# Both value-matmul groups of an attention unit placed side by side in layer 0

## Chip, cores, metric

One core of one Trainium2 chip runs the whole program. The metric is device time in microseconds (us), the median of several executions of one compiled kernel. The profile and the trace come from one execution, taken by the hardware profiler.

## What is computed

Two transformer layers with parallel branches, on x of 4 sequences x 256 tokens x 512 features, in float32:

```python
xn = layernorm(x)
x = x + attn0(xn) + ffn0(xn)      # 32 query heads, 8 key/value heads, head size 16, no mask
xn = layernorm(x)
x = x + attn1(xn) + ffn1(xn)      # same head layout, rotary positions, causal mask
```

`attn0` is softmax(q k^T / 4) v for every head, then a 512x512 output projection. The change touches only this attention.

## The kernel before

The four sequences are n = 0..3 in layer 0. The 32 heads of a sequence are cut into S = 4 slices of 8 heads, so layer 0 has 16 **units** u = 4n + s. A unit is worked in eight **slots**, i = 0..7. In slot i three things can stand on TensorE:

- `("st", u, i)`, L785: transposed scores of 128 keys against 2 heads x 256 queries, into PSUM bank `k % 3` (banks 0 to 2). ScalarE then writes exp of it to `probs[:, i]` (L953). Slots 0 to 3 hold the first 128 keys, slots 4 to 7 the second 128.
- `("m", u + 2, i)`, L752: scores of the unit two ahead, for the row maximum only. VectorE reduces them (`neg_max`, L1097). These scores go to one of the three work banks 3, 4, 5, which rotate among all short-lived products, so a matmul for a work bank waits until VectorE or ScalarE has read what stood there three products ago.
- one piece of **beside** work, from `beside_units`: projections of the next sequence (`qkv`), output projection of the previous one (`wo`), transposes of normalised input (`xn`), value transposes (`v`), and weight splits (`split`) on ScalarE and VectorE.

The **value matmuls** `("pv", u, t)`, L813, multiply `probs` by the values. Group t = 0 uses probs 0 to 3, group t = 1 uses probs 4 to 7; both accumulate in one bank, 6 or 7 by the parity of u. A group is four 128-row by 32-column matmuls on four column strips of the array, and float32 makes each two passes, so the trace counts 8. Before a group the program waits for the last exp that it reads. ScalarE's exps of unit u wait in turn for group t of unit u - 1, because they overwrite its `probs`:

```python
if u:
    act.wait_ge(pv_done, 2 * (u - 1) + t + 1)
```

Once per unit come two more small steps. `("mt", u + 1)`, L766, transposes the maxima, VectorE copies them (`max_t`, L1106), and a DMA (`mrow`, L554) puts them in a row of `big`, on which score step 0 of that unit waits. `("norm", u - 1, k)`, k = 0..3, in slots 4 to 7 on VectorE (L1113 o_tok, L1117 o_rec, L1122 o_div, L1129 o_t), divides by the softmax sum and turns the result; then ScalarE copies it to `ctxT` (L961) and GpSimd makes its low part (L646, `ctx_lo`). The output projection of sequence n - 1 stands in slots 0 to 6 of the sequence's second unit, and its first piece waits for the last unit of that sequence:

```python
pe.wait_ge(ctx_lo, S * (n + 1))
```

The order of all steps is one list, written by hand in `attention_order`; every engine walks the same list and carries out its own part in that order. Before the change, group 0 of a unit stands at the end of slot 7 of its own unit (`AT["pv0"] = (7, 6)`), and group 1 in slot 2 of the next unit (`AT["pv1"] = (2, 3)`). So TensorE's order at a unit's border is

```text
st7 m7 [pv u,0] beside | st0 m0 beside | st1 m1 beside | st2 m2 [pv u,1] mt beside | st3 ...
```

Units 14 and 15 have no `m` (there is no unit two ahead), and unit 15 carries first pieces of the feed-forward's up projection in slots 1 to 3. After unit 15 its two groups follow each other directly, then the rest of that projection.

Of the kernel before, what the change touches and what calls it, by code (L numbers as in the profile page):

```python
# [53 lines left out]
AT = {"pv1": (2, 3), "mt": (2, 2), "norm": (4, 3), "pv0": (7, 6), "v": (2, 5), "keys": (4, 2),  # L54
      "queries": (13, 14), "wo0": (8, 9), "wo1": (11, 10), "ln": (19, 21), "xn": (23, 23),
      "weights": ((19, 21, 23), (19, 21, 23)), "hidden": ((25, 3), (25, 5))}
# [3 lines left out]
def parts(x):  # L60


    count = KT * (x[1] + 1) if x[0] == "up" else 4
    return [("part", x, p) for p in range(count - 1)] + [x]
# [55 lines left out]
def beside_units(n, L):  # L120

    b = n - B * L
    more = b < B - 1
    at = {(s, i): [] for s in range(S) for i in range(8)}

    def place(first, steps):
        for k, x in enumerate(steps, first):
            at[k // 8, k % 8].append(x)  # L130

    if b > 0:
        place(AT["v"][L], [("v", n)])
    if more:
        place(AT["keys"][L], project(n + 1, 2))
        if b > 0:
            place(0, project(n + 1, 0)[2:])
            place(AT["queries"][L], project(n + 1, 1))
    if b > 0:

        place(AT["wo0"][L], parts(("wo", n - 1, 0)))
        place(AT["wo1"][L], parts(("wo", n - 1, 1)))
    if b + 2 < B:
        if n == 0:
            at[1, 4].append(("split", L, "attn", 3))
            at[2, 4].append(("split", L, "attn", 4))
        if b == 0:
            at[1, 0].append(("stats", L, 2))
            at[1, 2].append(("stats", L, 3))
            at[1, 5] += [("root", L, 2), ("root", L, 3)]  # L150
            at[1, 7] += [("rstd", L, 2), ("rstd", L, 3)]
        place(AT["ln"][L], [("ln", n + 2)])
        place(AT["xn"][L], transposed(n + 2))
        place(30, parts(("qkv", n + 2, 0))[:2])
    if not more:
        for at_, x in zip(AT["weights"][L], (("up", 0), ("up", 1), ("down", 0))):
            place(at_, [("split", L) + x])
        first, count = AT["hidden"][L]
        place(first, first_hidden(L)[:count])
    return at  # L160


def first_hidden(L):


    return parts(("up", L, 0)) + (parts(("up", L, 1)) if L == 0 else [])


def attention_order(L):

    n0, u0, u1 = B * L, B * S * L, B * S * (L + 1)
    o = []
    for u in range(u0, u1):
        n, s = divmod(u, S)
        b = n - n0
        more = b < B - 1
        if s == 0:
            beside = beside_units(n, L)
        for i in range(8):
            if i == 0:  # L180
                if s == 0 and b > 0:
                    o += [("load_ke", n, 1), ("load_q", n, 3)]
                if s > 1 and more:
                    o += [("load_q", n + 1, s - 1)]
                if s == 2 and more:
                    o += [("load_km", n + 1, 1), ("load_ke", n + 1, 0)]
                if s > 0 and not more:
                    o += [("load_xf", L, s - 1)]
            o += [("st", u, i)]
            if u + 2 < u1:  # L190
                o += [("m", u + 2, i)]
            if i == AT["pv1"][L] and u > u0:
                o += [("pv", u - 1, 1)]
            if i == AT["mt"][L] and u + 1 < u1:
                o += [("mt", u + 1), ("mrow", u + 1)]
            if i == 3 and s == 1 and more:
                o += [("load_km", n + 1, 0)]
            if i == 0 and s == 1 and more:
                o += [("load_q", n + 1, 0)]
            if 0 <= i - AT["norm"][L] < 4 and u > u0:  # L200
                o += [("norm", u - 1, i - AT["norm"][L])]
            if i == AT["pv0"][L]:
                o += [("pv", u, 0)]
            o += beside[s, i]
    o += [("load_xf", L, 3), ("pv", u1 - 1, 1)] + first_hidden(L)[AT["hidden"][L][1]:]
    o += [("norm", u1 - 1, k) for k in range(4)]
    o += [("hidden", L, 0), ("hidden_lo", L, 0), ("wo", n0 + B - 1, 0), ("wo", n0 + B - 1, 1)]
    return o + ([("up", L, 1)] if L == 1 else [])
# [47 lines left out]
def program_order():  # L256
    o = [("stats", 0, 0), ("root", 0, 0), ("rstd", 0, 0)] + attention_start(0)
    for L in range(2):
        o += attention_order(L) + ffn_order(L)
    return o  # L260
# [962 lines left out]
```

## Time and profile before

| | |
|---|---|
| runs shown | 662.39, 662.84, 664.12 us; median 662.84 |
| span of the profiled execution, first to last instruction | 661.3 us; the page gives no whole time of its own for it |
| mean granted TensorE clock | 0.977 |
| TensorE busy | 605.0 us (91%), weight loads 458.7 us |
| VectorE, ScalarE, GpSimd busy | 411.5, 298.9, 183.4 us |
| layer 0's units | about 46 to 211 us of the span |

Engines are called PE (TensorE matmul), PEld (its weight load), DVE (VectorE), ACT (ScalarE), POOL (GpSimd), SPq (the queue that issues DMAs). A bracket behind a row of the timeline is the idle time of that engine before it and what ended it. The chain of waits follows the work back from the last instruction, so a piece in it is one that the end had to wait for.

### The profile page before, as it was taken

How to read it: one execution, taken by the hardware profiler on the slowest of the kernel's cores; microseconds unless marked ns; L12 is line 12 of the kernel's file. 1: busy time of each engine (PE TensorE's matmuls, PEld its weight loads, DVE VectorE, ACT ScalarE, POOL GpSimd, SP SyncE). 2: the span in 40 equal slices, each digit the busy share in tenths (PEclk: the TensorE clock that was granted, in tenths of full speed). 3: DMA queues.
4: the chain of work that ended last, by engine and by line, in shares of the span. 5: the costliest groups of instructions: out<-in, count | busy, mean ns of one | idle time of the engine just before them, and what ended most of it. 6: DMA issues, size and time to landing. Idle time of an engine off the chain costs nothing.

```text
span 661.3 us, 10058 instructions
## 1 busy us (share of the span) xinstructions
PE 605.0 (91%) x3392; PEld 458.7 (69%) x3392; DVE 411.5 (62%) x750; ACT 298.9 (45%) x554; POOL 183.4 (28%) x296
## 2 busy tenths in 40 slices
PE   3778799999988999999989999989989989789997
PEld 2766467577554888888878888747667667458886
DVE  6676976866954444445556565797777686533343
ACT  2215564654636444455644433545444354542331
POOL 7400110121002122212123332335455464621100
PEclk9878899999989999999999999989999999899999
DMA  5679543564439244434343945345344355653321
GB/s 198 172 208 284 143 132 95 129 176 113 125 78 215 90 115 130 127 112 111 112 126 113 234 165 161 82 115 141 113 109 133 113 129 113 155 117 96 96 95 63
DMA packets 39882, 88.24 MB, mean 133 GB/s; under 512 B 4884, under 2 KB 25620, under 8 KB 36760
## 3 DMA queue, kind: packets, MB, share of 16 engines
q1 hardware_dynamic: 31480, 59.29, 33.5%
q0 software_dynamic: 8352, 28.32, 14.4%
q8 instruction: 27, 0.44, 0.3%
q14 instruction: 23, 0.19, 0.1%
HBM read 64.26 MB, written 23.07 MB: 132 GB/s over the span
## 4 chain that ended last, share of the span: by engine, by line
PE 74%; DVE 15%; issue 6%; ACT 3%; DMA 1%; POOL 1%; SPq 0%; DVEq 0%; ACTq 0%; POOLq 0%
PE banks L696 50%; PE banks L752 7%; PE banks L813 6%; DVE neg_max L1097 4%; PE banks L785 3%; PE banks L790 3%; PE banks L757 2%; DVE xn L1039 1%; DVE bn L1016 1%; PE banks L766 1%; DMA big<-q_parts 1%; ACT probs L953 1%; DVE rot_b L1066 1%; DVE o_tok L1113 1%; DVE o_t L1129 1%
## 5 line engine op out<-in xcount | busy, mean ns | idle before, releaser
L1097 DVE TENSOR_REDUCE neg_max<-banks 128x2 f32<-128x512 f32 (+1 forms) x256 | 152.7, 611 | 68.0 <-PE banks L757 36.8
L953 ACT ACTIVATE probs<-banks 128x512 f32<-128x512 f32 (+1 forms) x256 | 131.6, 547 | 95.4 <-PE banks L790 48.7
L696 PE MATMUL banks<-big,w_up 128*128 128x512 f32 x576 | 142.3, 394 | 0.8 <-issue 0.8
L696 PEld LDWEIGHTS banks<-big,w_up 128*128 128x128 f32 x576 | 107.8, 189 | 26.0 <-issue 4.1
L752 PE MATMUL banks<-k_max,big 96*128 96x256 f32 x512 | 109.9, 300 | 13.9 <-DVE neg_max L1097 8.4
L752 PEld LDWEIGHTS banks<-k_max,big 96*128 96x128 f32 x512 | 91.1, 196 | 35.1 <-DVE neg_max L1097 18.2
L696 PE MATMUL banks<-w_down,w_up 128*128 128x512 f32 x384 | 96.7, 394 | 1.6 <-DVE w_up L1153 1.6
L696 PE MATMUL banks<-xnT,w_qkv 128*128 128x256 f32 x576 | 89.1, 297 | 6.0 <-DVE w_qkv L1006 2.9
L696 PEld LDWEIGHTS banks<-xnT,w_qkv 128*128 128x128 f32 x576 | 78.8, 199 | 19.6 <-issue 9.8
L696 PEld LDWEIGHTS banks<-w_down,w_up 128*128 128x128 f32 x384 | 70.2, 188 | 15.6 <-DVE w_up L1006 2.0
L1006 DVE TENSOR_TENSOR w_up<-raw,w_up 128x512 fp32r<-128x512 f32 (+1 forms) x40 | 32.4, 810 | 73.8 <-ACT w_up L884 73.8
L630 POOL TENSOR_SCALAR_AFFINE_SELECT probs<-probs 128x256 f32<-128x256 f32 x128 | 57.8, 452 | 62.4 <-ACT probs L953 50.8
L813 PE MATMUL banks<-probs,v_sb 128*32 128x512 f32 (+1 forms) x512 | 63.4, 568 | 4.0 <-POOL probs L630 3.1
L696 PE MATMUL banks<-w_out,ctxT 128*128 128x512 f32 x192 | 53.9, 411 | 5.1 <-DVE neg_max L1097 3.8
L646 POOL TENSOR_TENSOR ctxT<-o_t,ctxT 128x256 fp32r<-128x256 f32 x32 | 23.7, 739 | 119.8 <-ACT ctxT L961 119.1
L584 POOL DMA_DIRECT2D raw<-in_down x40 | 22.0, 550 | 121.6 <-DVE w_up L1006 100.5
L785 PE MATMUL banks<-big,k_exp 96*128 96x512 f32 x128 | 53.1, 424 | 1.8 <-ACT probs L953 1.8
L790 PE MATMUL banks<-big,k_exp 96*128 96x512 f32 (+1 forms) x128 | 50.7, 402 | 2.1 <-ACT probs L953 1.9
L696 PEld LDWEIGHTS banks<-w_out,ctxT 128*128 128x128 f32 x192 | 34.2, 193 | 13.2 <-DVE neg_max L1097 4.3
L979 ACT ACTIVATE w_up<-banks,bias_up 128x512 fp32r<-128x512 f32 x32 | 22.1, 689 | 41.9 <-PE banks L696 41.7
L884 ACT CAST w_down<-raw 128x512 fp32r<-128x512 f32 x40 | 24.8, 621 | 35.4 <-PE banks L696 27.9
L584 POOL DMA_DIRECT2D raw<-in_up x40 | 22.6, 564 | 65.8 <-DVE w_down L1006 27.3
(84 smaller groups left out, 648.5 us busy)
## 6 DMA issues: line engine op xcount, KB each, us to landing
big<-q_parts SPq DMA_DIRECT2D x64, 256.0 KB, 4.3
raw<-in_down POOLq DMA_DIRECT2D x40, 256.0 KB, 2.9
xn_parts<-xnT SPq DMA_DIRECT2D x8, 1024.0 KB, 5.1
q_parts<-stage SPq DMA_DIRECT2D x32, 256.0 KB, 2.5
raw<-in_up POOLq DMA_DIRECT2D x32, 256.0 KB, 3.0
big<-xn_parts SPq DMA_DIRECT2D x16, 512.0 KB, 6.4
raw<-in_attn POOLq DMA_DIRECT2D x10, 512.0 KB, 4.2
k_parts<-stage SPq DMA_DIRECT2D x16, 256.0 KB, 2.7
```

Source lines behind the costliest of these rows:

```text
L584: pool.dma_start(raw[:, k % RAW, 0:n], src).then_inc(raw_loaded[k % RAW], 16)
L630: nc.gpsimd.affine_select(out=slot, in_=slot, compare_op=ALU.is_ge, fill=0.0, base=0, pattern=[[0, 2], [1, P]], channel_multiplier=-1).the ...
L646: nc.gpsimd.tensor_tensor(ctxT[:, 1, s, :], o_t[:, :], ctxT[:, 0, s, :].bitcast(F32), ALU.subtract).then_inc(ctx_lo, 1)
L696: mm = nc.tensor.matmul(out_ap, lhs(a), rhs(b_), start=first and j == 0, stop=last and j == 2, **kw)
L752: mm = nc.tensor.matmul(banks[:, k, r * T:r * T + T], big[0:ROWS, s, 2 * g + r, t * P:t * P + P], k_max[0:ROWS, 4 * f + g, :], start=r == ...
L785: mm = nc.tensor.matmul(bank, keys, big[0:ROWS, s, 2 * g:2 * g + 2, :], start=True, stop=True)
L790: mm = nc.tensor.matmul(part, keys, big[0:ROWS, s, 2 * g:2 * g + 2, q0:], start=True, stop=True)
L813: mm = nc.tensor.matmul(o, v_sb[:, t, 4 * f + g, :], p_, start=t == 0, stop=t == 1, skip_group_check=True)
L884: nc.scalar.copy(to[0], raw[:, k % RAW, 0:n]).then_inc(hi_split, 1)
L953: nc.scalar.activation(probs[:, i, 0:w], banks[:, k % 3, 0:w], ACT.Exp, scale=SCALES[n // B]).then_inc(exp_done, 1)
L1006: nc.vector.tensor_tensor(to[1], raw[:, k % RAW, 0:n], to[0].bitcast(F32), ALU.subtract).then_inc(lo_split, 1)
L1097: nc.vector.tensor_reduce(neg_max[:, s, t, 2 * g:2 * g + 2], banks[:, work_bank(x), :].rearrange("p (r t) -> p r t", r=2)[:, :, 0:w], AX.X ...
```

## The change

In layer 0 both groups of unit u - 1 stand in slot 1 of unit u, directly behind its second score step and the maximum step beside it. Group 0 thus moves from the end of slot 7 to two slots later, group 1 from slot 2 to one slot earlier. The last unit keeps its two groups behind its slot 7, and layer 1 keeps its places. No instruction is added or removed, and no DMA is moved past another. The new order at a border is

```text
st7 m7 beside | st0 m0 beside | st1 m1 [pv u,0] [pv u,1] beside | st2 m2 mt beside | st3 ...
```

```diff
@@ attention_order
             if u + 2 < u1:
                 o += [("m", u + 2, i)]
-            if i == AT["pv1"][L] and u > u0:
+            if L == 0 and i == 1 and u > u0:
+                o += [("pv", u - 1, 0), ("pv", u - 1, 1)]
+            if L == 1 and i == AT["pv1"][L] and u > u0:
                 o += [("pv", u - 1, 1)]
...
-            if i == AT["pv0"][L]:
+            if L == 1 and i == AT["pv0"][L]:
                 o += [("pv", u, 0)]
             o += beside[s, i]
-    o += [("load_xf", L, 3), ("pv", u1 - 1, 1)] + first_hidden(L)[AT["hidden"][L][1]:]
+    o += [("load_xf", L, 3)] + [("pv", u1 - 1, 0)] * (L == 0) + [("pv", u1 - 1, 1)] + first_hidden(L)[AT["hidden"][L][1]:]
```

## Rows read from the trace of the kernel before

**Rows 1.** The page's chain of waits by engine, shares of the span.
```profile
PE 74%; DVE 15%; issue 6%; ACT 3%; DMA 1%; POOL 1%; SPq 0%; DVEq 0%; ACTq 0%; POOLq 0%
```

**Rows 2.** Windows: us, busy of PE, PEld, DVE, ACT, POOL, then clock, DMA, GB/s.
```profile
57.00:88.00 31.00, 24.80 (x144) 13.96 (x142) 27.27 (x60) 19.65 (x38) 3.33 (x5) 0.94 0.58 154
...
103.00:121.00 18.00, 17.94 (x113) 13.22 (x112) 11.02 (x20) 8.75 (x18) 2.91 (x4) 1.00 0.44 111
...
163.00:184.00 21.00, 18.70 (x123) 11.16 (x116) 19.52 (x40) 13.37 (x28) 3.47 (x4) 0.99 0.56 138
```

**Rows 3.** Chain of waits, in order of time: start us, us, what.
```profile
100.83 1.00 PE banks L813 x8
101.83 0.91 PE banks L696 x6
102.73 0.23 PE banks L785
...
103.21 0.06 issue
103.26 0.94 PE banks L696 x3
...
106.83 0.31 PE banks L766 x2
...
117.46 0.72 PE banks L696 x6
...
174.04 0.43 PE banks L785
```

**Rows 4.** Timeline, 101 to 103 us: start us, us, engine and instruction.
```profile
101.47 0.43 DVE L1129 STREAM_TRANSPOSE o_t<-o_div 128x256 f32<-128x256 f32 x1
...
101.94 0.41 ACT L961 CAST ctxT<-o_t 128x256 fp32r<-128x256 f32 x1 [0.71 <-DVE o_t L1129]
102.42 0.74 POOL L646 TENSOR_TENSOR ctxT<-o_t,ctxT 128x256 fp32r<-128x256 f32 x1 [5.59 <-ACT ctxT L961]
```

**Rows 5.** Timeline, 162 to 178 us, units with little beside work.
```profile
162.46 1.29 DVE L1097 TENSOR_REDUCE neg_max<-banks 128x2 f32<-128x512 f32 x2 [0.50 <-PE banks L752]
...
168.88 0.50 PE L752 MATMUL banks<-k_max,big 96*128 96x256 f32 x2
169.11 1.84 DVE L1097 TENSOR_REDUCE neg_max<-banks 128x2 f32<-128x512 f32 x3
...
169.31 1.07 PE L813 MATMUL banks<-probs,v_sb 128*32 128x512 f32 x8
...
173.76 0.63 DVE L1097 TENSOR_REDUCE neg_max<-banks 128x2 f32<-128x512 f32 x1
...
175.59 1.85 DVE L1097 TENSOR_REDUCE neg_max<-banks 128x2 f32<-128x512 f32 x3
```

**Rows 6.** Timeline, 183 to 184 us, start of the third output projection.
```profile
183.01 0.72 POOL L646 TENSOR_TENSOR ctxT<-o_t,ctxT 128x256 fp32r<-128x256 f32 x1 [6.10 <-ACT ctxT L961]
...
183.84 1.62 PE L696 MATMUL banks<-w_out,ctxT 128*128 128x512 f32 x3 [2.30 <-DVE neg_max L1097]
```

**Rows 7.** Window behind that wait, columns as in rows 2.
```profile
184.00:186.00 2.00, 2.00 (x6) 1.61 (x7) 0.00 (x0) 0.08 (x1) 0.00 (x0) 0.50 0.78 168
```

**Rows 8.** Timeline, 201 to 211 us, units 14 and 15.
```profile
201.19 1.06 PE L813 MATMUL banks<-probs,v_sb 128*32 128x512 f32 x8
...
203.13 0.70 PE L785 MATMUL banks<-big,k_exp 96*128 96x512 f32 x2 [0.87 <-ACT probs L953]
...
208.89 2.11 PE L813 MATMUL banks<-probs,v_sb 128*32 128x512 f32 x16
```

**Rows 9.** Chain of waits, where it passes to VectorE behind unit 0.
```profile
60.29 0.69 DVE neg_max L1097
```

**Rows 10.** Timeline, 74 and 83 us, in units 2 and 3.
```profile
74.67 0.38 PE L766 MATMUL banks<-ident,neg_max 128*8 128x128 f32 x2 [1.67 <-DVE neg_max L1097]
...
83.18 0.66 PE L718 MATMUL banks<-ident,xn 128*128 128x128 f32 x4 [0.42 <-DVE neg_max L1097]
```

## The prediction

> **What bounds the kernel now.** I read the page first. TensorE is on the chain that ends last for most of the span and VectorE for much of the rest [rows 1]. That is an average, so I cut layer 0's units into stretches by the window view. Three kinds appear. In units with much beside work TensorE is full and VectorE has a third of its time free (second row of [rows 2]). At the start (57 to 88 us) and in units 10 to 12, which have almost no beside work, VectorE is busy 88 to 93% of the time and TensorE nearly as much (first and third row). In units 14 and 15 exps and a DMA of maxima set the pace. A group of value matmuls costs TensorE 1.00 us wherever it stands [rows 3]. So the change is not about its work but about what the 1.00 us covers at its old place and uncovers at its new one. For that I followed the chain of waits border by border and then read, in the timeline, what each wait at a border was for. There are 16 pairs; I call the pair of unit u "pair u". It now stands in slot 1 of unit u + 1.
>
> **What moving costs TensorE itself.** Nothing is added. After a group the next wide matmul's weight load is not hidden: six projection matmuls take 0.91 us behind a group and 0.72 elsewhere, a lone score step 0.43 instead of the usual 0.23 [rows 3]. So an exit costs 0.19 to 0.20 us. Before, group 0 has such an exit and group 1 leads into `mt`, whose narrow weight load costs less (0.31 us against an estimated 0.22 if hidden). After, there is one exit of 0.20. That saves about 0.08 us. The trace has one pair already, behind unit 15: 16 matmuls take 2.11 us where one group takes 1.06 [rows 8]. There the second group's exp ended just as it started, so 1.04 us for a second group is an upper bound. The lower bound is one without any gap between groups, which I put at 0.86 us, an estimate from the 1.06 less the 0.20 that an exit shows. I take 1.00. Where TensorE is the bound (pairs 3, 7, 13) the change is then worth -0.1 us each, and -0.25 at the lower bound.
>
> The Trainium skill says on its page TensorEngine Tiling (Array Packing), Key Properties, that changing the tiling mode drains TensorE. The 0.19 us exit fits that. If a switch were all that mattered, a rule of "fewer switches" would make this change a gain; that is the second rival below.
>
> **Borders where the output projection starts (pairs 4, 8, 12).** Take unit 4's border. Its slot 7 contains group 0 at 100.83 to 101.83. Then come 0.91 us of projection, a score step and a maximum step, and at 103.21 the first piece of the output projection waits 0.06 us [rows 3]. It waits for the previous sequence's last context: VectorE's o_t at 101.47 to 101.90, ScalarE's copy to 102.35, GpSimd to 103.16 [rows 4]. That chain hangs on the last maximum step, which stands ahead of group 0 in both orders, so it doesn't move. Without group 0, TensorE reaches this wait 1.00 + 0.19 us earlier, at about 102.0, and stands until 103.2. Behind the wait it then has a pair instead of one group: 1.04 us for the second group and 0.20 for the exit, less 0.09 at `mt`, some +1.2 us. Queued behind this wait are score step 1, so ScalarE's exps too, but they have slack. Unit 8's border repeats the pattern one sequence later (wait also 0.06 us), and at unit 12's border TensorE already waits 2.30 us for the same chain at 183.84 [rows 6]; there again group 0 was covered and no longer is. Sum: 3 x 1.2 = +3.6 us. Bounds: at least 3 x 0.9, if the pair gains 0.14 inside and a little elsewhere; at most 3 x 1.2 plus a clock effect (third rival).
>
> **Units with little beside work (pairs 9 to 11).** VectorE has no idle time here: from one slot-2 burst of reductions to the next it takes 175.59 - 169.11 = 6.48 us per unit [rows 5]. It keeps busy through a group's 1.00 us because up to three products wait in the three work banks. A pair is twice as long. The maximum step of slot 1 needs the bank of slot 6, whose reduction ends at 173.76 + 0.63 = 174.39. From there VectorE has work until the second reduction of the next burst ends, at 175.59 + 1.23 = 176.82: 2.43 us. TensorE needs from the same moment 0.05 us reaction, 0.43 for the maximum step up to the group's start (168.88 to 169.31) [rows 5], 2.04 for the pair, 0.43 + 0.24 for the next score and maximum step [rows 3], some 3.2 to 3.3 us. VectorE idles 0.8 us per unit, so a unit takes 7.3. Written out: the slot-2 reduction of unit 10 starts at 162.46 + 0.61 = 163.1 before and 0.9 later after, because group 1 now stands ahead of it. The next two stand at 170.3 and 176.8 before [rows 5], and at 171.3 and 178.6 after. That is +1.8 us on VectorE's chain that leads to GpSimd's context at 183.01 and to the wait behind it [rows 6]. Bounds: 0.5 (if only one unit starves) to 2.2.
>
> **Start (pairs 0 to 2) and pairs 5, 6.** Pair 0: TensorE's chain runs through group 0 and the 0.91 exit into VectorE, which from 60.29 on is the chain [rows 9]. Without group 0, VectorE gets that product 1.2 us earlier. It then meets a hole of about 0.2 us for the slot-2 product before `max_t`: -1.0 us, which lasts as long as VectorE stays the bound, to 88 us. Bounds -1.2 to 0. Pair 1: VectorE is behind by several products, 0. Pairs 2 and 6: the pair now stands ahead of the second transposes of `xn` (83.18), which start 1.5 us later [rows 10]; ScalarE copies and VectorE drains them only two slots on. `mt` no longer has group 1 right ahead of it. Balance on the drain +0.3 us each, bounds 0 to 1. Pair 5: VectorE becomes the bound just behind it and gets the slot-2 product 0.9 us later, partly made good: +0.3. Sum -1.0 + 0.9 = -0.1 us.
>
> **Pair 14.** Before, group 0 of unit 14 runs at 201.19 while TensorE waits anyway until 203.13 for unit 15's scores [rows 8]. After, it stands behind the second of these, in the part where score steps and up projection fill TensorE up to the last pair: +1.0 us, bounds 0.6 to 1.2. Pair 15 doesn't move.
>
> **ScalarE.** Exp 0 of the next unit now waits for group 0, about 2 us later than before. Score step 3 needs that exp; between them stand group 1 (1.00) and score and maximum step 2, and an exp takes some 0.6 us. This cover is enough; without it each unit would lose up to 0.6 us.
>
> **The sum.** -0.3 + 3.6 + 1.8 - 0.1 + 1.0 = +6.0 us. The profiled span of 661.3 would become 667.3. The measured median lies 1.5 above that span, so I add the sum to the median: 668.8 us. Everything behind layer 0's attention only shifts.
>
> **Rivals.**
> - *Cover lost only at fixed chains.* Work banks carry VectorE through the pair, since the hole of 0.8 us rests on a hand schedule; then the 1.8 and 0.9 fall away: +3.3 us, 666.1, and 665.0 with the pair gaining inside. For it: VectorE's idle brackets in rows 5 are small and rest on modelled ends. Against it: 2.43 us of stock against 3.2 us of hole. Chance 0.18.
> - *Fewer switches win (the other side).* The context chain is late for another reason than group 0's place, or the wait at the borders is refilled, so that nothing waits there, and each of 15 borders saves 0.08 + 0.14 = 0.2 us with unit 0's -1.0: -4 at best, -1 to -3 likely, about 660.8. It decides if the wait at 103.2 moves forward with TensorE, that is if o_t hung on group 0. In the order it doesn't. Chance 0.08.
> - *The clock falls too.* Behind the 2.30 us wait the granted clock is 0.50, the 1.2 GHz level [rows 6, 7], and three output matmuls take 1.62 us against 0.94 at unit 4's border [rows 3]. If the new 1.2 us waits at units 4 and 8 did the same, each would cost some 1.5 to 2.5 us, a pair in it another 0.9: +9 to +11 us, 672.5. Against: behind a wait of 1.67 us at 74.67 two `mt` matmuls take their usual 0.38 us [rows 10]. Chance 0.07.
> - *No net change.* All moves hide in slack, within 0.3% (2.0 us, about what this measurement can tell from nothing): 662.8. For it: only 15 us of value matmuls are moved in all. Chance 0.07.
> - My forecast, 667 to 670.5: chance 0.60.
>
> Low end: the first rival with the pair's inner gain, 664.8. High end: every bound at its top (3.8 + 2.2 + 1.9 + 1.2 = 9), 671.5. Slower by over 0.3% takes the forecast, the clock and nearly all of the first rival: 0.83. Within 0.3%: 0.09. Faster: 0.08.
>
> **What would show it.** In the changed profile: an idle of about 1.2 us of TensorE ahead of the first output projection in units 5 and 9, and over 2.3 in unit 13; pieces of 16 value matmuls of about 2.05 us; VectorE idle of about 0.8 us ahead of the slot-2 reduction in units 11 and 12, released by L752; VectorE's first reduction of unit 1 at about 59.1 instead of 60.29; unit 15's last group ending 6 us later than 210.9. The prediction is wrong if the output projection starts without such waits, if 16 matmuls take under 1.9 us, or if exps hold up score step 3.

## The result and the profile after

The changed kernel takes 676.5 us (median of 4 runs, 675.22 to 679.18) against 663.5 us for the kernel before beside it (4 runs, 662.39 to 667.46): a ratio of 1.0192 with the interval [1.0155, 1.0228]. It is slower by 1.9%, some 13 us, where +6.0 us was forecast; the time also lies above the predicted range. The profiled execution spans 677.5 us, 16.2 more than before's 661.3.

The page's busy times and its chain by engine:

```profile
PE 614.3 (91%) x3392; PEld 466.0 (69%) x3392; DVE 412.0 (61%) x750; ACT 299.2 (44%) x554; POOL 183.4 (27%) x296
...
PE 72%; DVE 13%; issue 6%; DMA 4%; ACT 3%; POOL 1%; SPq 0%; DVEq 0%; ACTq 0%; POOLq 0%
```

Against [rows 1], DMA has gone from 1 to 4% of the chain, and VectorE from 15 to 13%. These shares count the whole time of a transfer on the chain and not what it costs. But no DMA was moved, so a wait for a transfer that other work had covered is the first thing to look for. TensorE is busy 614.3 us where the page of before has 605.0, with the same 3392 instructions: part of the loss is matmuls that take longer.

To find the places I took one mark in each unit, the start of its slot 7's exp, and compared by how much the distance from unit to unit grew. The same kernel was run a second time (label after_again). These are worked out from the two traces, in us; "step" is the growth in the unit in which the pair now stands:

| pair (step in unit) | forecast | changed kernel | the same, again |
|---|---|---|---|
| none (up to unit 0) | 0 | +0.49 | +0.12 |
| 0 (1) | -1.0 | -1.17 | -1.17 |
| 1 (2) | 0 | +3.05 | +2.49 |
| 2 (3) | +0.3 | +2.64 | +1.20 |
| 3 (4) | -0.1 | +0.51 | +0.51 |
| 4 (5) | +1.2 | +0.97 | +0.97 |
| 5, 6 (6, 7) | +0.6 | +0.35 | +1.87 |
| 7 (8) | -0.1 | +0.50 | +0.51 |
| 8 (9) | +1.2 | +0.97 | +0.96 |
| 9 to 11 (10 to 12) | +1.8 | +1.64 | +1.63 |
| 12 (13) | +1.2 | +1.84 | +2.12 |
| 13 (14) | -0.1 | -0.21 | -0.21 |
| 14 (15) | +1.0 | +2.50 | +2.37 |
| sum | +6.0 | +14.08 | +13.37 |

The remaining 2 us of the span's 16.2 lie behind layer 0's attention, where nothing was changed and single executions differ from each other. Windows of the changed kernel, two as in [rows 2] and three more:

```profile
57.00:88.00 31.00, 22.18 (x123) 13.63 (x125) 25.28 (x55) 16.93 (x31) 3.33 (x5) 0.80 0.63 155
...
103.00:121.00 18.00, 16.77 (x108) 13.48 (x107) 10.90 (x21) 7.28 (x15) 1.47 (x2) 1.00 0.34 104
184.00:209.00 25.00, 21.81 (x120) 13.70 (x122) 16.07 (x31) 9.88 (x19) 1.46 (x2) 0.86 0.33 73
...
86.00:88.00 2.00, 2.00 (x12) 0.39 (x8) 1.15 (x2) 0.21 (x1) 0.16 (x1) 0.50 0.03 8
196.00:198.00 2.00, 2.00 (x14) 0.50 (x16) 0.69 (x1) 0.00 (x0) 0.00 (x0) 0.50 0.00 0
```

The 31 us at the start have a granted clock of 0.80 where they had 0.94, and every engine but GpSimd has done less in them. From 103 to 121 us nothing is lost to the clock (1.00). From 184 to 209 us it is 0.86, where the same window of the kernel before has 0.94. The 2 us windows from 86 and 196 us show the low level, 0.50 or 1.2 GHz; both lie within a pair of value matmuls, as the chain shows:

```profile
60.91 0.38 SPq L527
61.33 6.53 DMA k_parts<-stage
67.88 4.36 DMA k_max<-k_parts
72.37 0.77 PE banks L754 x2
...
73.99 2.77 PE banks L815 x16
...
85.79 3.57 PE banks L815 x16
...
97.47 1.85 PE banks L815 x16
99.32 0.92 PE banks L698 x6
...
100.75 0.60 ACT qkv_v L914
101.39 0.44 PE banks L739 x2
...
108.77 0.94 PE banks L698 x3
...
110.18 1.85 PE banks L815 x16
...
193.79 1.62 PE banks L698 x3
195.41 0.43 PE banks L787
196.26 3.08 PE banks L815 x16
...
214.68 0.70 PE banks L787 x2
215.38 3.16 PE banks L815 x16
```

Line numbers are two above those of before (L815 is the old L813, the value matmul), in the runs further down one to three above. What to read here: a pair is 1.85 us long where the granted clock is 2.4 GHz, and 2.77, 3.57, 3.08 and 3.16 us in units 2, 3, 13 and 15. These four cost 12.58 - 4 x 1.85 = 5.2 us. Each stands right behind a place where TensorE waits (3.74, 1.83, 2.76 and 1.82 us), and the pieces ahead of it are long too (three output matmuls 1.62 for 0.94 at 193.79, a score step 0.43 for 0.23). The first three rows are the wait that the forecast lacks; the timeline has it as an idle time, and beside it the waits that were forecast:

```profile
59.60 0.69 DVE L1099 TENSOR_REDUCE neg_max<-banks 128x2 f32<-128x512 f32 x1 [0.50 <-PE banks L754]
...
72.37 0.77 PE L754 MATMUL banks<-k_max,big 96*128 96x256 f32 x2 [3.74 <-DMA k_max<-k_parts]
...
108.77 0.94 PE L698 MATMUL banks<-w_out,ctxT 128*128 128x512 f32 x3 [1.23 <-DVE neg_max L1099]
...
179.47 0.69 DVE L1099 TENSOR_REDUCE neg_max<-banks 128x2 f32<-128x512 f32 x1 [0.66 <-PE banks L754]
...
186.69 0.69 DVE L1099 TENSOR_REDUCE neg_max<-banks 128x2 f32<-128x512 f32 x1 [0.66 <-PE banks L754]
```

### The profile page after: what moved, and what is told of

It is laid out like the page before. It is cut to its first block, busy times and chain, and to the rows that moved or that the text cites. A ratio compares the mean times of both kernels' runs of the same rounds, so it can differ in the third digit from the quotient of the medians.

```text
span 677.5 us, 10058 instructions
## 1 busy us (share of the span) xinstructions
PE 614.3 (91%) x3392; PEld 466.0 (69%) x3392; DVE 412.0 (61%) x750; ACT 299.2 (44%) x554; POOL 183.4 (27%) x296
## 4 chain that ended last, share of the span: by engine, by line
PE 72%; DVE 13%; issue 6%; DMA 4%; ACT 3%; POOL 1%; SPq 0%; DVEq 0%; ACTq 0%; POOLq 0%
PE banks L698 47%; PE banks L815 8%; PE banks L754 7%; DVE neg_max L1099 3%; PE banks L792 3%; PE banks L787 3%; PE banks L759 2%; PE banks L720 1%; DMA k_parts<-stage 1%; DVE xn L1041 1%; DVE bn L1018 1%; DMA big<-q_parts 1%; PE banks L768 1%; DVE o_tok L1115 1%; DVE rot_b L1068 1%
## 5 line engine op out<-in xcount | busy, mean ns | idle before, releaser
L754 PEld LDWEIGHTS banks<-k_max,big 96*128 96x128 f32 x512 | 92.9, 199 | 37.8 <-DVE neg_max L1099 18.7
L698 PE MATMUL banks<-xnT,w_qkv 128*128 128x256 f32 x576 | 90.5, 301 | 5.4 <-DVE xnT L1047 2.6
L698 PEld LDWEIGHTS banks<-xnT,w_qkv 128*128 128x128 f32 x576 | 80.9, 204 | 14.8 <-issue 4.9
L815 PE MATMUL banks<-probs,v_sb 128*32 128x512 f32 (+1 forms) x512 | 66.9, 621 | 4.0 <-POOL probs L632 3.1
L792 PE MATMUL banks<-big,k_exp 96*128 96x512 f32 (+1 forms) x128 | 52.1, 413 | 0.6 <-issue 0.3
```

The source lines that it names most:

```text
L698: mm = nc.tensor.matmul(out_ap, lhs(a), rhs(b_), start=first and j == 0, stop=last and j == 2, **kw)
L754: mm = nc.tensor.matmul(banks[:, k, r * T:r * T + T], big[0:ROWS, s, 2 * g + r, t * P:t * P + P], k_max[0:ROWS, 4 * f + g, :], start=r == ...
L792: mm = nc.tensor.matmul(part, keys, big[0:ROWS, s, 2 * g:2 * g + 2, q0:], start=True, stop=True)
L815: mm = nc.tensor.matmul(o, v_sb[:, t, 4 * f + g, :], p_, start=t == 0, stop=t == 1, skip_group_check=True)
```

## The experiments

Most kernels move only some pairs. They share one edit of the kernel before, with the moved units in a tuple:

```diff
+            if i == 1 and L == 0 and u - 1 in MOVED:
+                o += [("pv", u - 1, 0), ("pv", u - 1, 1)]
-            if i == AT["pv1"][L] and u > u0:
+            if i == AT["pv1"][L] and u > u0 and not (L == 0 and u - 1 in MOVED):
                 o += [("pv", u - 1, 1)]
...
-            if i == AT["pv0"][L]:
+            if i == AT["pv0"][L] and not (L == 0 and u in MOVED):
                 o += [("pv", u, 0)]
```

Ratios are to runs of the kernel before on the same chip (medians 663.5 to 665.0 us in the four batches), with their 95% intervals; 0.1% is 0.66 us.

### Which of the two groups costs the time

after_again is the changed kernel as it stands.

> The changed kernel once more, as control for what differs from one execution to the next. If the 6.5 us that the store of k_parts took behind unit 0 belongs to the change, unit 2's first maximum step again waits until about 72 us and the time is again 675 to 678 us. If it was chance of one execution, the store lands in about 4.5 us, unit 2 comes 2 to 3 us earlier and this profile is at 673 to 675 us. If the stretches at 1.2 GHz follow from TensorE's waits they stand at the same borders (units 2, 3, 13, 15); if they are chance they stand elsewhere.

Measured: 677.1 us, 1.018 [1.0162, 1.0197]; the steps are in the table above. So the places of the loss are those of the kernel. Units 3 and 7 differ between the two executions by 1.4 and 1.5 us in opposite directions.

g0_only moves group 0 to slot 1 and leaves group 1 in slot 2, so no two groups follow each other:

```diff
+            if L == 0 and i == 1 and u > u0:
+                o += [("pv", u - 1, 0)]
             if i == AT["pv1"][L] and u > u0:
                 o += [("pv", u - 1, 1)]
...
-            if i == AT["pv0"][L]:
+            if i == AT["pv0"][L] and (L == 1 or u == u1 - 1):
```

> Half of the change: group 0 in slot 1 of the next unit, group 1 stays in slot 2. Theory of place (group 0 no longer covers waits at the unit's border, and the exps wait for it): nearly the whole loss, +10 to +13 us. Theory of length (two groups in a row starve VectorE and stretch the slow-clock stretches): with a score and a maximum step between the groups most of it is gone, +3 to +6 us.

Measured: 677.3 us, 1.0182 [1.0158, 1.0206].

g1_only moves group 1 alone, to slot 1:

```diff
-"pv1": (2, 3)
+"pv1": (1, 3)
```

> The other half: group 1 one slot earlier, in slot 1, group 0 stays at the end of slot 7. Theory of place: group 1 covers nothing different, -0.5 to +1 us. Theory of length doesn't apply here, it expects the same; if this alone costs over 2 us, group 1's place matters and both theories miss something.

Measured: 664.0 us, 0.998 [0.9961, 1.0].

By the times, the whole loss comes with group 0's place. Group 1's is worth nothing in sum, or a gain of 0.2% at the interval's edge, and that two groups stand next to each other costs nothing that these runs can measure, some 0.3%. Unit by unit group 1's place is not free: units 4 and 8 grew by 0.83 us each in g1_only and by -0.01 and -0.02 in g0_only. What it uncovers there is read below, at full_only. In unit 15 g0_only grew by 0.75, where the changed kernel grew by 2.50.

### The wait ahead of the output projection

late_wo is the changed kernel with the first piece of the output projection one slot later, behind the pair instead of ahead of it:

```diff
-"wo0": (8, 9), "wo1": (11, 10)
+"wo0": (9, 9), "wo1": (11, 10)
```

> The changed kernel with the first half of the output projection one slot later (slots 9 to 12, second half unchanged 11 to 14), so that in units 5 and 9 the pair itself stands ahead of its first piece. Theory of place: the new waits of 1.2 us at these two borders are covered again, and part of the long wait in unit 13: -2.4 to -4 us against the changed kernel, 672.5 to 674. If the waits at the borders were only moved slack, no difference, 676.5.

Measured: 670.2 us, 1.0066 [1.0042, 1.0091]. From the steps: unit 5 -0.11 (it was +0.97), unit 9 -0.12, unit 13 -2.94 (it was +1.84), unit 15 +2.32 as ever. The chain of this kernel in unit 5, then in unit 13:

```profile
106.98 1.85 PE banks L816 x16
108.83 0.90 PE banks L699 x3
...
190.61 0.94 PE banks L699 x3
```

The output matmuls follow the pair with no idle time, and those of unit 13 take 0.94 us again where the changed kernel's took 1.62. So 2 x 1.1 us are the two borders' waits. At unit 13 the wait ahead of these matmuls has gone from 2.76 to 0.22 us and the low clock behind it is gone too, 4.8 us with what was there before. That does not show the second to follow from the first: in start_only and pair1 TensorE waits the same 2.30 us there as in the kernel before, and the matmuls behind take 0.93 and 0.94 us with no low clock. What is left of the loss by the steps is 2.7 us in units 1 to 3, 2.3 in unit 15, 1.6 in units 10 to 12 and 1.0 in units 4 and 8, less the 2.9 of unit 13.

before_late_wo makes the same edit in the kernel before, to see whether that is a gain of its own.

> The kernel before with only the first half of the output projection one slot later (9 to 12). In unit 13 TensorE waits 2.3 us for the last context ahead of that piece and its clock falls behind it. With a score and a maximum step, which need no context, ahead of the wait, VectorE gets a product earlier and the wait shrinks: -1.5 to -3 us against before. If the wait is only moved one slot on: 0.

Measured: 664.1 us, 1.0003 [0.9982, 1.0023]: a miss, no gain. In its trace the clock falls at 185.5 us although the wait ahead of it is shorter (1.83 for 2.30 us). In the kernel before group 0 covers that wait up to 0.06 us at two of the three borders, so the later place buys little there; with group 0 gone it is worth 7 us (677.1 to 670.2).

### The pairs one set at a time

start_only, wo_borders, light_only, full_only and end_only are the shared edit with MOVED set to (0, 1, 2), (4, 8), (9, 10, 11), (3, 7, 13) and (12, 13, 14).

> Only pairs 0, 1 and 2 are placed as in the change, all else as before. The prediction gave this part -0.7 us. The changed kernel's profile says otherwise: unit 2 waits for the load of k_max, whose store can't land earlier than the transfers ahead of it, and a pair falls into the stretch at 1.2 GHz: +2 to +4 us, most of it by unit 3. If the excess there came from chance of one execution: -1 to +0.5 us.

Measured: 666.6 us, 1.0054 [1.0033, 1.0074]. Steps: unit 1 -1.18, unit 2 +2.28, unit 3 +1.21. In its chain, unit 2 and unit 3:

```profile
73.01 3.42 PE banks L816 x16
...
85.20 2.45 PE banks L816 x16
```

The gain of pair 0 is there to 0.2 us and is more than lost one unit on.

> Only pairs 4 and 8, at the borders where the output projection starts. Theory of place: +1.0 us each as the profile after shows (predicted 1.2), so +2 us. If this part were hidden by VectorE's slack behind it: +0 to +0.7 us.

Measured: 665.1 us, 1.0021 [1.0002, 1.0039]. Steps: unit 5 +0.96, unit 9 +0.97, no other of units 1 to 15 by more than 0.25. The clock stays at 2.4 GHz behind both waits.

> Only pairs 9, 10 and 11, in the units with little beside work. Theory of the hole (VectorE runs out of products while TensorE does the pair): +1.5 to +1.8 us. If three work banks carry VectorE through, as the first rival has it: 0 us.

Measured: 666.5 us, 1.0047 [1.0027, 1.0067]. Steps: +0.26, +0.52, +0.88, together 1.66. VectorE in its timeline:

```profile
170.91 0.69 DVE L1100 TENSOR_REDUCE neg_max<-banks 128x2 f32<-128x512 f32 x1 [0.67 <-PE banks L755]
...
178.14 0.69 DVE L1100 TENSOR_REDUCE neg_max<-banks 128x2 f32<-128x512 f32 x1 [0.67 <-PE banks L755]
```

Its slot-2 burst, one run of three in [rows 5], is broken by an idle time of 0.67 us, and from one to the next it takes 178.14 - 170.91 = 7.23 us (6.48 before, 7.3 forecast). The ratio's 3.1 us is more than the 1.66 that the steps show; the lower edge of the interval, 1.8, is near them.

> Only pairs 3, 7 and 13, where TensorE is the bound. Prediction: -0.3 us, up to -0.75 with the inner gain of a pair. The profile after shows a new wait instead in units 4 and 8: the copies of a projection and of v_t stand on ScalarE behind exps that now wait for group 0, and the value transposes wait for them. By that, +0.5 us each for pairs 3 and 7 and -0.2 for pair 13: +0.8 us.

Measured: 665.7 us, 1.0024 [1.0002, 1.0047]. Steps: unit 4 +0.50, unit 8 +0.51, unit 14 -0.21; unit 13 too grew by 1.37, with a longer stretch at 1.2 GHz in this execution. A loss, where -0.3 was forecast. The chain behind pair 3:

```profile
92.85 1.85 PE banks L816 x16
...
96.13 0.60 ACT qkv_v L915
96.78 0.44 PE banks L740 x2
```

The pair is at its short 1.85 us, and still the chain leaves TensorE for ScalarE's copy of the values (L915), for which the value transposes (L740) wait. The expectation blamed the moved group 0, for which exps queued ahead of that copy wait. The traces say otherwise. In the kernel before, group 1 stood in slot 2 between the projection and these transposes, and there was no wait; g1_only takes it away from there and leaves group 0, g0_only does the reverse. The kernel before, then g1_only and g0_only:

```profile
94.83 0.99 PE banks L813 x8
95.82 0.31 PE banks L766 x2
96.14 0.22 PE banks L737 x2
...
98.70 0.44 PE L737 MATMUL banks<-ident,v_t 128*128 128x128 f32 x2 [0.47 <-ACT qkv_v L912]
...
98.47 0.38 PE L739 MATMUL banks<-ident,v_t 128*128 128x128 f32 x2
```

The wait of 0.47 us is there wherever group 1 has left slot 2 (also in the changed kernel, and with 0.48 in slot0 and slot7) and is missing where it has stayed. So what came into the open in units 4 and 8 is what group 1 covered, ScalarE's copy of the values. The copy cannot come sooner, since it needs the projection that TensorE does in slot 1: in full_only ScalarE stands 0.59 us for that projection right ahead of its copies. Between 57 and 225 us the changed kernel's ScalarE does idle 26.8 us in 12 exps that wait for value matmuls; that this costs time is not shown.

> Only pairs 12, 13 and 14. Prediction: +2.1 us (1.2 in unit 13, 1.0 in unit 15, -0.1). Theory of the clock on top: each of the two pairs falls into a stretch at 1.2 GHz and takes about 3.1 us instead of 1.85, so +4 to +5 us in all. The difference tells the clock's share apart.

Measured: 668.8 us, 1.0078 [1.005, 1.0105]. Steps: unit 13 +1.06, unit 14 -0.20, unit 15 +2.76. Its chain and one window in unit 15:

```profile
186.01 2.26 PE banks L816 x16
...
204.01 1.19 PE banks L788 x2
205.20 2.90 PE banks L816 x16
```

```profile
206.00:208.00 2.00, 2.00 (x16) 0.38 (x8) 0.00 (x0) 0.81 (x2) 0.46 (x1) 0.68 1.03 225
```

The score step takes 1.19 us for the 0.70 of [rows 8], the pair 2.90 for 1.85, and the clock granted within it averages 0.68: part of the pair runs at 1.2 GHz.

Added up, these five give 0.54 + 0.21 + 0.47 + 0.24 + 0.78 = 2.2% (pair 13 is in two sets, pairs 5 and 6 are in none), where the whole change costs 1.8 to 1.9%. Each term is uncertain by 0.2 to 0.3%, the sum by some 0.5%. Within that the sets explain the loss and do not act on each other.

### Two pairs alone

pair1 and pair14 move one pair each.

> Only pair 1. The prediction gave it 0. Theory of the covered transfer: group 0 of unit 1 runs before while TensorE has to wait for the load of k_max anyway, and stands behind this wait after, at 1.2 GHz: +1.5 to +2.5 us, most of the +3.2 of the run with pairs 0 to 2. If that loss comes from pair 2 and the transposes of xn instead: 0 to +0.5.

Measured: 665.3 us, 1.0014 [0.999, 1.0038]; step of unit 2 +1.30. By the time alone this is inconclusive, since the interval holds no change; the step is plain. The chain in unit 2:

```profile
60.91 4.59 DMA k_parts<-stage
65.52 4.14 DMA k_max<-k_parts
...
71.41 3.18 PE banks L816 x16
```

With pair 0 back in its old place, TensorE still waits for the transfer in unit 2, 2.79 us, and the pair behind it again runs slow.

> Only pair 14. Prediction: +1.0 us. The run with pairs 12 to 14 shows it with a pair of 2.90 us in a stretch at 1.2 GHz, and +2.8 us between units 14 and 15. If the clock falls here also with this pair alone: +2 to +3 us. If not, +1 us and a pair of 1.9 us, which tells the clock's part of the price.

Measured: 666.2 us, 1.0028 [1.0001, 1.0055]; step of unit 15 +2.58, forecast +1.0. The chain:

```profile
202.04 0.70 PE banks L788 x2
202.74 3.29 PE banks L816 x16
```

### Other places for the pair

slot0 puts each pair into slot 0 of the next unit, one slot earlier than the change. The MOVED edit holds for all 15, with `i == 0` for `i == 1`.

> All 15 pairs side by side, but in slot 0 instead of slot 1, so ahead of the first piece of the output projection. Theory of place: the waits in units 5, 9 and 13 are covered again, exps and the copies behind them are held one slot less; the load of k_max (unit 2) and of the maxima (unit 15) still stand ahead of the pair: +6 to +8 us against before, where the changed kernel had +13. Theory of length (two groups in a row are what costs): +11 to +13 again.

Measured: 667.8 us, 1.0058 [1.0039, 1.0077]. Steps: unit 2 +2.35, unit 3 +2.62, unit 15 +1.95, unit 13 -2.50 (some 1.4 of it because its trace has no low clock there, see below). One slot back and two thirds of the loss are gone, but not the three places where TensorE waits right ahead of the pair.

slot7 leaves group 0 where it was and brings group 1 to it, at the end of slot 7 of its own unit; slot7_part does so for nine of the pairs.

```diff
+BOTH = tuple(range(15))            # slot7_part: (0, 3, 4, 5, 7, 8, 12, 13, 14)
...
-            if i == AT["pv1"][L] and u > u0:
+            if i == AT["pv1"][L] and u > u0 and not (L == 0 and u - 1 in BOTH):
                 o += [("pv", u - 1, 1)]
...
-                o += [("pv", u, 0)]
+                o += [("pv", u, 0)] + [("pv", u, 1)] * (L == 0 and u in BOTH)
```

> All pairs at the end of slot 7 of their own unit: group 0 stays where it was and group 1 comes to it. Theory of place: nothing is uncovered at any border, and a pair saves 0.2 us of TensorE; only the units with little beside work lose through the longer hole: -2 to +1 us against before. Theory of length: +5 us or more.

Measured: 661.2 us, 0.9957 [0.9936, 0.9978]. This beats both kernels, and not by the clock: the mean over its 12 runs, 0.971, is that of the kernel before. Steps: unit 4 +0.47, unit 5 -0.52, unit 13 -2.49. Its chain at the border of unit 4 and, further on, at unit 13:

```profile
100.48 1.85 PE banks L814 x16
102.34 0.91 PE banks L697 x6
...
182.62 0.93 PE banks L697 x3
```

The pair of 1.85 us stands where the wait of [rows 4] is to be covered and is followed by the projection with no idle time. At unit 13 the output matmuls take 0.93 us behind 1.44 us of waiting, where before they took 1.62 behind 2.30 us [rows 6]; as in slot0, some 1.4 of the 2.49 us is low clock that this trace lacks.

> Pairs at the end of slot 7 only for units 0, 3, 4, 5, 7, 8, 12, 13 and 14; the other units as before. Theory of place: nine pairs at -0.2 us and no hole in the units with little beside work, -1 to -3 us against before and at least as fast as with all pairs moved. Theory of length: +3 us or more.

Measured: 662.4 us, 0.9971 [0.9952, 0.9991]. A gain on the kernel before. At least as fast as with all pairs was expected; it is no faster, and the two intervals overlap.

no_clock_borders is the change without pairs 1, 2, 12 and 14, those behind which the clock was low.

> The change in slot 1 without pairs 1, 2, 12 and 14. If those four hold the whole excess over the forecast, what is left is the forecast of the rest: 1.2 x 2 + 1.8 - 1.0 + 0.6 - 0.3 = +3.5 us. With the two corrections that the runs showed (no gain from pair 0, 0.5 us each for pairs 3 and 7): +5.5 us. More than +7 us would mean that the excess is spread over all borders.

Measured: 670.8 us, 1.0084 [1.0054, 1.0115], +5.6 us. Leaving four of 15 pairs alone takes away over half of the loss of 1.8 to 1.9%. What is left is larger than the +3.5 us of the forecast's own terms and agrees with the +5.5 that the measured steps of the single sets give. Its trace also has pair 0 moved with pair 1 in its old place: unit 1 -1.17, unit 2 +1.49.

## Why the forecast fell short

**What held.** The direction, and that group 0 and not the pairing is the cost. The waits ahead of the output projection: 1.23 us measured at 108.77, some 1.2 forecast, and +0.97 per border, since the pair gave back 0.15 inside. The units with little beside work: VectorE idles 0.66 us twice, 0.8 forecast, and they cost 1.64 us, 1.8 forecast; 2.43 us of stock do not carry it through the longer hole. Pair 0: -1.17, forecast -1.0, seen as VectorE's reduction at 59.60 instead of 60.29. Pairs 5 and 13 to 0.1 us each. The first rival needed the light units to cost nothing, the second the wait to move with TensorE; both are excluded. The exit cost of 0.19 to 0.20 us stands as well (projection 0.92 and 0.91 behind a pair). The Trainium skill's page TensorEngine Tiling (Array Packing), Key Properties, says that a change of tiling mode drains TensorE. The trace agrees with it, though no run here shows that the exit is this drain. What fewer exits would save, 0.2 us at a border, is less than any cover that was lost.

**The step that failed: "Pair 1: VectorE is behind by several products, 0."** In unit 2, TensorE needs k_max, a load that hangs on another transfer. In the kernel before, its issue is here (the last row is a window, columns as in [rows 2]):

```profile
61.59 0.90 SPq L525 DMA_DIRECT2D k_parts<-stage  x2
...
66.28 0.50 SPq L548 DMA_DIRECT2D k_max<-k_parts  x1
...
68.04 1.94 PE L813 MATMUL banks<-probs,v_sb 128*32 128x512 f32 x8
...
68.00:70.00 2.00, 2.00 (x10) 0.30 (x9) 2.00 (x4) 1.99 (x3) 0.58 (x1) 0.50 0.93 258
```

and the first maximum step of unit 2 starts at 70.49, 4.2 us behind that issue. The trace has this load land 3.6 us behind its issue, at 69.8. Group 0 of unit 1 stood at 68.04, in that gap, and no wait was printed there. I read VectorE's stock and never asked which transfer ended just ahead of the step. With group 0 moved behind, TensorE stands 3.74 us at 72.37 and still has the pair to do. pair1 shows it alone, +1.30 us. The same rows contradict the premise of the whole forecast, that a group costs TensorE "1.00 us wherever it stands": this one took 1.94, with the clock at 0.50, in a gap where that cost nothing.

**Pair 0's gain was not kept.** Its term was right, and "lasts as long as VectorE stays the bound, to 88 us" was wrong. The store of k_parts is issued at 60.91 instead of 61.59, and the load of k_max at 67.88 instead of 66.28: the second part of the store took 6.53 us to land, before 4.2. In all seven traces with group 0 of unit 0 moved it took 5.2 to 6.5 us, in those without 2.5 to 4.6 (pair1 4.59) but for 6.3 in before_late_wo. In no_clock_borders, where pair 1 did not move, the 1.17 us gained in unit 1 are followed by +1.49 in unit 2. Work finished sooner ahead of a transfer is no gain if the transfer does not end sooner.

**The clock, put at nothing in the sum.** The third rival had the mechanism and named units 4 and 8, where it did not happen in either trace of the change. It happened at units 2, 3, 13 and 15, and I took the pair's cost for 2.04 us everywhere. In the kernel before, group 0 ran ahead of or within those waits, where its length cost nothing (1.94 us at unit 2, 1.06 or 1.07 at the other three); now the pair stands right behind, where TensorE's clock is low: 2.77, 3.57, 3.08 and 3.16 us. So pair 14's term was +1.0 and measured +2.3 to +2.8 in five traces, pair 2's +0.3 and measured +1.2 to +2.6, pair 12's +1.2 and measured +1.06 to +2.1.

What the low clock costs can be read from traces that differ in it at one place. With nothing moved there, unit 13 is 1.4 us shorter in start_only and pair1, which have no low clock in it, than in the kernel before, which has it from 183.5 to 186.9 us, and 1.4 us longer in full_only, where it lasts twice as long. Unit 3 with pair 2 moved grew by 2.64 and by 1.20 to 1.26 us, unit 7 by 0.08 and 1.60, again with one such stretch more or less. In unit 15 all six traces with the pair moved into it have a low stretch and grew by 1.95 to 2.76; g0_only has none and grew by 0.75. The places alone thus cost near what was forecast: 1.06 at unit 13 (end_only, with as much low clock as before; 1.2 forecast) and some 0.75 at unit 15 (group 0 alone, g0_only; 1.0 forecast). Over the whole program the mean granted clock is 0.962 in eight executions of the changed kernel and 0.971 in 100 of the kernel before. That is some 13 us more at the low level, worth 5 to 6 of the 13 us lost, an estimate from 1.4 us for each 3.4 us stretch. The forecast had this term at nothing, on the strength of one wait of 1.67 us without a fall.

**Pairs 3 and 7.** "Where TensorE is the bound the change is worth -0.1 us each": the inner cost of a second group is 0.85 us (1.85 - 1.00), the lower bound that I did not take, and still each cost +0.5. The paragraph on ScalarE asked whether exps are in time for score step 3, and nothing asked what group 1 covered in slot 2. It covered the copy of the value projection, for which TensorE's transposes wait.

**A slip in the range.** The bounds at their top add up to 9.1 us, which makes the high end 671.9 and not 671.5. The measured 676.5 lies above both.

**The account.** Of the 8.1 us between the steps' 14.1 and the forecast's 6.0: 5.4 in units 2 and 3, 1.2 at pairs 3 and 7, 1.5 at pair 14, 0.6 at pair 12, 0.5 ahead of any moved pair, less some 1.1 where the forecast was too high (borders, light units, pairs 0, 5, 6 and 13).

**What stays open.** How unit 2 divides between place and clock. Its clock is low in the kernel before too, for half as long. Inside the pair the low clock explains at most 2.77 - 1.85 = 0.9 of the 3.05 us, the rest being wait and slower steps beside it. In slot7 the pair ahead of that place took 3.8 us at the low clock and unit 2 grew by 0.00. Nor is it shown what makes the clock fall behind one wait and not behind another of the same length. Stretches at 1.2 GHz begin at other times in other executions of one kernel, and the changed kernel has two traces here and every other kernel one. Nor is it shown that the earlier store of k_parts was slowed by other transfers; the traces only show that it took longer.

## What to carry to other kernels

A work item that stands where its engine would otherwise wait is free there and costs its full time elsewhere, and while it stands there the trace shows no wait at all: before moving one, look up what the next instructions depend on, transfers and copies on other engines, and when each of them ended. Do this for every item that moves: group 1, which seemed to cover nothing, covered 0.5 us twice. Two items that do belong together are better joined at the place that covers a wait (0.9957 here) than behind it (1.0192). Price what lands behind a wait at the low clock too.

## What the hardware showed beside that

- Two groups of value matmuls in a row, with their inputs ready, take 1.85 us at 2.4 GHz, one alone 1.00. A second group thus costs 0.85, where [rows 8] had made it 1.04; there its input came late.
- The same pair takes from 2.26 to 3.57 us behind a wait in the chains shown, in stretches granted 1.2 GHz in whole or in part (0.50 at 86 and 196 us in the changed kernel, 0.68 at 206 us in end_only). TensorE had waited 3.74 us ahead of the one at 73.99. Behind the 1.23 us wait at 108.77 the window of the stretch keeps 1.00.
- The clock's low stretches stand at other places in other executions, and single executions of the kernel before lie between 659.8 and 668.3 us. A change of 0.2% could be told only by 12 runs, and by the steps of a trace only in units whose clock is the same in both traces.
